# A cross-attention and FP4 feed-forward kernel: P times V as two stacked products, and the last steps written out in an order of their own

## The chip, the cores and the metric

One Trainium2 chip, one core of it. The metric is the device time of one execution in microseconds (us); of the kernel before there are three timed runs. Engines are named as in the profile: PE is TensorE (PEld its loads of stationary operands), DVE is VectorE, ACT is ScalarE, POOL is GpSimd, and SP is SyncE, which here issues nearly all DMAs.

## What is computed

x is 4 x 2048 x 512, the context 4 x 77 x 512. The inputs are float32.

```python
x = x + xattn(layernorm(x), ctx, ctx, mask)       # 16 heads of 32, 77 keys
#   q = x Wq.T + bq; k = ctx Wk.T + bk; v = ctx Wv.T + bv
#   probs = softmax(where(mask, q k.T / sqrt(32), -1e9)); attn = probs v; out = attn Wo.T + bo
x = x + ffn(layernorm(x))
#   fp4_linear quantizes both operands in blocks of 16 along the last axis to FP4 (E2M1)
#   h = silu(fp4_linear(x, w_gate)) * fp4_linear(x, w_up); out = fp4_linear(h, w_down)   # inner width 1408
```

## The kernel before

The 8192 rows of x are cut into 64 tiles of 128 rows. Everything of one tile is done in one pass through seven stages, and seven tiles are in flight at a time: step(e, d, f, a, b, n, m) handles tile s+4 as m (first norm), s+3 as n (queries, scores, softmax), s+2 as b (P times V), s+1 as a (output projection, residual, second norm, quantizing), s as f (gate and up products), s-1 as d (quantizing of h) and s-2 as e (down product and output). In this text step s is the one in which f is tile s.

float32 operands of a product are split in two bf16 halves, HI and LO, and each product is made of three: HI x HI, HI x LO, LO x HI (PRODUCTS). The halves are written by ACT (a copy, HI) and DVE (a subtraction, LO), and turned by a DMA transpose that SP issues.

P times V of a tile is weighted_values(b) on PE. For each of the 16 heads the stationary operand is pT, 77 rows (keys) by 128 columns (queries), and the moving one is 33 columns of v_cur: 32 of V and one of ones, which gives the sum of the row of P. Three matmuls a head make 48 a tile. Its result is in banks 2 to 5, which are also used by the scores and by the third gate/up chunk (banks 2 and 3). DVE reads it in sums_inverse and normalised.

Order of PE in a step: P times V of b, queries of n (48 matmuls), clear_scores, gate/up chunk 0 of f, scores of n, projection of a, down of e, gate/up chunks 1, 2 and 3 of f. Gate/up chunk 0 needs xqT, the turned quantized input of tile f; that is one buffer, so the transpose for the next tile is issued by SP only when chunk 3 of the present one is done (xq_transposed waits for gu_ps). hT, the turned h, is one buffer as well: h_transposed waits for down_done of the tile before.

Each engine has its own instruction list, written out by hand and synchronised by semaphores; within an engine the order of the list holds. Steps 1 to 3 and the last six are unrolled, the others run in a loop (tiles()). In the steps 61 to 65, which have no new tile to take in, the same step function runs with the missing stages left out. A prologue before the steps quantizes the weights, makes K and V and starts the first tiles. V of each of the 4 batches goes to a DRAM scratch and comes back into v_cur at the first step of a batch (load_values), K at the last step of the batch before (load_keys).

Of the kernel before, what the change touches and what calls it, by code (L numbers as in the profile page):

```python
# [11 lines left out]
U32 = mybir.dt.uint32  # L12
# [52 lines left out]
def xattn_fp4_ffn_kernel(nc, x, ctx, mask, wq, bq, wk, bk, wv, bv, wo, bo, w_gate, w_up, w_down, out):  # L65
# [11 lines left out]
    V_LOADS = 16  # L77
# [17 lines left out]
    v_scratch = nc.dram_tensor("v_scratch", [BATCH, KEYS, 2 * D], BF16, kind="Internal").ap()  # L95
    x1_scratch = nc.dram_tensor("x1_scratch", [TILES, P, D], F32, kind="Internal").ap()

    with ExitStack() as es:
# [25 lines left out]
        v_cur = sb("v_cur", [P, 2, HEADS, VW + 1], BF16)  # L124
# [20 lines left out]
        probs = sb("probs", [P, HEADS, KEYS])  # L145
# [29 lines left out]
        w_size, c_size, k_size, v_size = 2 * KC * D, 2 * KC * BATCH * KEYS, BATCH * 2 * GROUPS * KEYS, BATCH * 2 * D  # L175
        ends = [0]
        for size in (w_size, w_size, c_size, k_size, v_size, w_size):
# [5 lines left out]
        v_all = v_room[0:KEYS].rearrange("p (b s d) -> p b s d", b=BATCH, s=2)  # L183
# [21 lines left out]
         s_ps, s_max, exp_done, p0_hi, p1_hi, p0_lo, p1_lo, pv_done, o_ready, o_hi, o_lo, o_ps, x1_done,  # L205
# [3 lines left out]
                 "s_ps s_max exp_done p0_hi p1_hi p0_lo p1_lo pv_done o_ready o_hi o_lo o_ps x1_done "  # L209
# [5 lines left out]
        pT_loaded, p_hi, p_lo = (pT0_loaded, pT1_loaded), (p0_hi, p1_hi), (p0_lo, p1_lo)  # L215
# [32 lines left out]
        DRAIN = TILES + 2  # L248
# [29 lines left out]
        def _(sp):  # L278
# [9 lines left out]
            def load_values(b):  # L288

                sp.dma_start(v_cur[0:KEYS, :, :, 0:DK].rearrange("p s h d -> p (s h) d"),  # L290
                             v_scratch[bass.ds(b, 1)].rearrange("a k (n d) -> (a k) n d", d=DK)).then_inc(v_loaded, 16)
# [15 lines left out]
            sp.dma_start(v_scratch.rearrange("b p w -> p b w"), v_all.rearrange("p b s d -> p b (s d)")).then_inc(kv_stored, 16)  # L307
# [43 lines left out]
            def probabilities(n, pair):  # L351
                after(p_lo[pair], n + 1)
                after(pv_done, GH * n)
                transposed(pT[:, pair].rearrange("p s h t -> p (s h) t"),
                           p_h[:, pair].rearrange("p s w -> p (s w)"), pT_loaded[pair])
# [15 lines left out]
            def xq_transposed(a):  # L371
                after(xq_lo, a + 1)
                after(gu_ps, a * CHUNKS)
                transposed(xqT.rearrange("p s k t -> p (s k) t"), xq_h.rearrange("p s d -> p (s d)"), xqT_loaded)

# [110 lines left out]
            for n in range(TILES - 2, DRAIN + 3):  # L486
                step(n, n - first)
            sp.wait_ge(out_stored, 16 * TILES)

        @block.gpsimd  # L490
        def _(pool):
# [3 lines left out]
            own.did(pool.memset(v_cur[:].rearrange("p s h w -> p (s h w)").bitcast(U32), 0))  # L495
            own.did(pool.memset(probs[:], 0.0))
            own.did(pool.memset(p_h[:].rearrange("p a s w -> p (a s w)").bitcast(U32), 0))
            own.after()
            own.did(pool.memset(v_cur[:, HI, :, DK], 1.0))
# [106 lines left out]

        @block.tensor
        def _(pe):
# [74 lines left out]
            def weighted_values(b):  # L683

                pe.wait_ge(pT0_loaded, 16 * b + 16)
                pe.wait_ge(pT1_loaded, 16 * b + 16)
                for g in range(GROUPS):
                    for s, t in PRODUCTS:
                        for r, ps in enumerate(head_ps):

                            head = g * GH + r
                            ins = pe.matmul(ps[:, g * VW:(g + 1) * VW], pT[0:KEYS, head // PAIR, s, head % PAIR, :],  # L692
                                            v_cur[0:KEYS, t, head, 0:VW], start=s == t, stop=s == LO)
                            if g == GROUPS - 1 and s == LO:
                                ins.then_inc(pv_done, 1)
# [133 lines left out]

        @block.scalar  # L830
        def _(act):
# [19 lines left out]
            for kind, what in plan:  # L851
                if kind == "quant":
                    continue
                if kind == "round":
                    for half in range(2):
                        weight_grid(half, HALF, 2 * what + half + 1)
                    continue
                ps = bank[n % 8]
                act.wait_ge(prep_ps, n + 1)
                if kind == "weight":  # L860
                    which, dst, kc = what
                    ins = act.activation(dst[:, HI, kc, :], ps[:], ACT.Copy, scale=fill_scale[which])
                elif kind == "ctx":
                    ins = act.copy(ctxT[:, HI, what], ps[:, 0:BATCH * KEYS])
                elif kind == "keys":
                    if what == 0:
                        act.wait_ge(bk_ready, 1)
                    ins = act.activation(k_all[:, :, HI, what, :],
                                         ps[:, 0:BATCH * KEYS].rearrange("p (b k) -> p b k", b=BATCH),
                                         ACT.Identity, bias=bk_col[:, what:what + 1])  # L870
                elif kind == "values":
                    ins = act.copy(v_all[:, what, HI], ps[0:KEYS, :])
# [41 lines left out]
            def probabilities_high(n, pair):  # L914
# [3 lines left out]
                         probs[:, pair * PAIR:(pair + 1) * PAIR, :])\  # L918
                   .then_inc(p_hi[pair], 1)

# [52 lines left out]
            def step(e, d, f, a, b, n, m):  # L973
# [14 lines left out]
                if n is not None:  # L988
                    exponentials_second(n, range(2))
                    probabilities_high(n, 0)  # L990
                    exponentials_second(n, range(2, GROUPS))
                if a is not None:
                    normed_second(a)
                if n is not None:
                    probabilities_high(n, 1)
                if f is not None:
# [42 lines left out]
            probabilities_high(0, 0)  # L1039
            masked(1)  # L1040
# [5 lines left out]
            probabilities_high(0, 1)  # L1046
            gate_up_grid(6, 0)
# [7 lines left out]
            probabilities_high(1, 0)  # L1055
            gate_up_grid(7, 0)
            probabilities_high(1, 1)
            q_high(2)
# [16 lines left out]
            probabilities_high(2, 0)  # L1075
            gate_up_high(8, 1)
# [9 lines left out]
            probabilities_high(2, 1)  # L1086
            masked(3)
# [5 lines left out]
            probabilities_high(3, 0)  # L1093
            probabilities_high(3, 1)
            silu_chunk(0, 0)
# [10 lines left out]
            tiles(act, step)  # L1106

        @block.vector
        def _(dve):
# [82 lines left out]
            for kind, what in plan:  # L1192
# [23 lines left out]
                elif kind == "values":  # L1216
                    low(v_all[:, what, LO], ps[0:KEYS, :], v_all[:, what, HI], prep_lo, n + 1)
# [85 lines left out]
            def probabilities_low(n, pair):  # L1303
                dve.wait_ge(p_hi[pair], n + 1)
                high, whole = (p_h[:, pair, HI].rearrange("p (h k) -> p h k", k=P)[:, :, 0:KEYS],
                               probs[:, pair * PAIR:(pair + 1) * PAIR, :])
                low(p_h[:, pair, LO].rearrange("p (h k) -> p h k", k=P)[:, :, 0:KEYS], whole, high,
# [216 lines left out]


# [25 lines left out]
```

## Time and profile before

| | |
|---|---|
| median of 3 runs | 2054.94 us (2054.4 to 2055.07) |
| the profiled execution, its own time | 2054.96 us |
| its span, first to last instruction | 2053.1 us |
| mean granted PE clock | 0.971 |
| busy: PE, PEld, DVE, ACT, POOL | 94%, 59%, 86%, 58%, 22% |
| steps 5 to 60, one step | 28.91 us |
| P times V records (48 a tile) | 87.5 us in all |

The span is 1.9 us shorter than the execution's own time; what lies around it is taken as unchanged. Records of PE are modelled at their ends, so the distance between the starts of two groups is the better measure of what the first one costs.

### The profile page before, as it was taken

To read this page: it belongs to the slowest core of one execution; us is meant where nothing else is said; L and a number is where in the kernel's file an instruction comes from. 1 tells how busy PE (TensorE), PEld (TensorE's weight loads), DVE (VectorE), ACT (ScalarE), POOL (GpSimd) and SP (SyncE) were. 2 spreads that over 40 slices of the span, in tenths; PEclk is the share of its full clock that TensorE was granted. 3 is DMA by queue.
4 is the path that set the end of the run, shared out by engine and by line. 5 is a ranking of instruction groups with operands and counts; after the bars stand their busy time and mean duration, and the time that the engine had idled before them with its cause. 6 is when DMAs were issued, how large, how long until landed. Compare 5 with 4: busy or idle time off the path is not lost.

```text
span 2053.1 us, 50510 instructions
## 1 busy us (share of the span) xinstructions
PE 1931.9 (94%) x18816; PEld 1215.5 (59%) x18816; DVE 1771.6 (86%) x2676; ACT 1198.6 (58%) x2485; POOL 453.2 (22%) x525
## 2 busy tenths in 40 slices
PE   6447999999999999999999999999999999999986
PEld 4235566666666666666666666666666666666543
DVE  7898988888888888888888888988888888888873
ACT  4565665566656665566656665566556665566421
POOL 5563221112211221112111221122111221122110
PEclk9668999999999999999999999999999999999998
DMA  5354566655665556655765566555765566555632
GB/s 168 104 115 99 117 124 148 133 127 131 147 142 124 131 132 146 132 130 128 151 136 124 132 137 146 127 131 127 155 132 125 131 141 145 123 131 124 137 75 54
DMA packets 725826, 264.95 MB, mean 129 GB/s; under 512 B 677682, under 2 KB 678706, under 8 KB 725786
## 3 DMA queue, kind: packets, MB, share of 16 engines
q1 hardware_dynamic: 724202, 264.43, 58.4%
q8 instruction: 23, 0.38, 0.1%
q10 hardware_dynamic: 1584, 0.01, 0.1%
q14 instruction: 17, 0.14, 0.0%
HBM read 65.97 MB, written 34.82 MB: 49 GB/s over the span
## 4 chain that ended last, share of the span: by engine, by line
PE 86%; DVE 6%; DMA 3%; issue 2%; POOL 1%; SPq 1%; ACT 0%; DVEq 0%; POOLq 0%; another core or an unknown queue 0%; ACTq 0%
PE psum L679 43%; PE psum L615 38%; PE psum L692 3%; PE psum L721 2%; DVE h_room L1146 1%; DMA t_room<-halves 1%; DMA ph_room<-h_room 1%; POOL h_room L521 1%; PE psum L710 1%; DVE w_sc L1126 1%; DMA ph_room<-p_h 1%; POOL h_room L525 1%; DVE h_room L1188 1%; DVE wguT L1114 1%; SPq L336 0%
## 5 line engine op out<-in xcount | busy, mean ns | idle before, releaser
L679 PE MATMUL psum<-wguT,t_room 128*128 128x352 bf16 x6144 | 939.6, 313 | 15.9 <-DMA t_room<-halves 10.6
L679 PEld LDWEIGHTS psum<-wguT,t_room 128*128 128x128 bf16 x6144 | 596.3, 98 | 344.2 <-DMA t_room<-halves 10.4
L615 PE MATMUL psum<-wdT,ph_room 128*128 128x512 bf16 x2112 | 471.4, 382 | 13.0 <-DMA ph_room<-h_room 13.0
L542 POOL TENSOR_TENSOR ln_var_eps<-ln_mean_var,eps 128x1 f32<-128x1 f32 x128 | 105.2, 822 | 1198.4 <-DVE ln_mean_var L1261 1011.0
L615 PEld LDWEIGHTS psum<-wdT,ph_room 128*128 128x128 bf16 x2112 | 207.8, 98 | 266.5 <-issue 21.3
L895 ACT ACTIVATE silu_g<-psum 128x352 f32<-128x352 f32 x256 | 117.7, 460 | 421.3 <-PE psum L679 421.3
L901 ACT ACTIVATE probs<-psum,neg_max 128x77 f32<-128x77 f32 x1024 | 245.1, 350 | 3.8 <-DVE neg_max L1299 3.0
L1293 DVE TENSOR_TENSOR h_room<-silu_g,psum 128x352 f32<-128x352 f32 x256 | 132.4, 517 | 80.3 <-ACT silu_g L895 80.3
L926 ACT ACTIVATE t_room<-psum,bq_col 128x128 bf16<-128x128 f32 x256 | 73.2, 368 | 207.1 <-PE psum L615 207.0
L615 PE MATMUL psum<-t_room,wqT 128*128 128x128 bf16 x3072 | 186.7, 222 | 0.2 <-DMA t_room<-halves 0.2
L615 PE MATMUL psum<-woT,t_room 128*128 128x512 bf16 x768 | 179.8, 384 | 1.2 <-DMA t_room<-halves 1.2
L615 PEld LDWEIGHTS psum<-t_room,wqT 128*128 128x128 bf16 x3072 | 176.9, 99 | 0.6 <-issue 0.2
L839 ACT ACTIVATE h_sq<-h_room 128x1408 bf16<-128x1408 f32 (+2 forms) x94 | 108.2, 1151 | 113.0 <-DVE h_room L1146 113.0
L556 POOL TENSOR_TENSOR io_room<-io_room,bo_all 128x512 f32<-128x512 f32 x64 | 83.2, 1300 | 248.1 <-DMA io_room<-in_x_dram 248.1
L1314 DVE TENSOR_TENSOR x_new<-psum,io_room 128x512 f32<-128x512 f32 x64 | 44.3, 692 | 88.2 <-PE psum L615 75.0
L615 PEld LDWEIGHTS psum<-woT,t_room 128*128 128x128 bf16 x768 | 70.8, 99 | 83.4 <-issue 3.9
L1146 DVE SCALAR_TENSOR_TENSOR h_room<-h_room,h_sc 128x1408 f32<-128x1408 f32 x64 | 104.0, 1625 | 2.2
L1160 DVE TENSOR_TENSOR h_room<-h_room,h_sc 128x1408 f32<-128x1408 f32 x64 | 104.0, 1625 | 2.2
L546 POOL TENSOR_SCALAR ln_shift<-ln_mean_var,ln_rstd 128x1 f32<-128x1 f32 x128 | 101.9, 796 | 12.6
L1152 DVE SCALAR_TENSOR_TENSOR h_room<-h_sq,h_room 128x1408 f32<-128x1408 bf16 x64 | 102.0, 1593 | 2.9 <-ACT h_sq L839 2.9
L1114 DVE TENSOR_TENSOR h_room<-h_room 128x1408 bf16<-128x1408 f32 x64 | 103.6, 1619 | 0.0
L1156 DVE SCALAR_TENSOR_TENSOR h_room<-h_sq,h_room 128x1408 f32<-128x1408 bf16 x64 | 103.6, 1618 | 0.0
(103 smaller groups left out, 2459.3 us busy)
## 6 DMA issues: line engine op xcount, KB each, us to landing
io_room<-in_x_dram SPq DMA_DIRECT2D x128, 256.0 KB, 2.8
x_scratch<-x_new SPq DMA_DIRECT2D x64, 256.0 KB, 2.0
x_cur<-x_scratch SPq DMA_DIRECT2D x64, 256.0 KB, 3.0
out_dram<-io_room SPq DMA_DIRECT2D x64, 256.0 KB, 2.4
t_room<-halves SPq DMA_TRANSPOSE x192, 3.2
raw<-in_L_ffn_w_down_dram SPq DMA_DIRECT2D x4, 704.0 KB, 4.2
raw<-in_L_ffn_w_gate_dram SPq DMA_DIRECT2D x11, 256.0 KB, 2.6
raw<-in_L_ffn_w_up_dram SPq DMA_DIRECT2D x11, 256.0 KB, 2.9
```

Source lines behind the costliest of these rows:

```text
L542: own.did(pool.tensor_tensor(var_eps, mean_var[:, 1:2], eps[:], ALU.add))
L615: ins = pe.matmul(dst, left(i), right(j), start=first and n == 0, stop=last and n == len(PRODUCTS) - 1)
L679: ins = pe.matmul(ps[:, 0:CW], left[:, i, kc, :], wguT[:, which, j, kc, cols], start=(kc == 0 and i == j), stop=(kc == KC - 1 and i == LO))
L839: act.activation(dst, val, ACT.Square, scale=GRID_SLOPE).then_inc(done, 1)
L895: act.activation(silu_g[:, c % 2, :], gate_ps[c][:, 0:CW], ACT.Silu).then_inc(silu_done, 1)
L901: ins = act.activation(probs[:, h, 0:KEYS], score_ps[:, r, g, :], ACT.Exp, bias=neg_max[:, h:h + 1])
L1114: return own.did(dve.tensor_tensor(dst, ps, high, ALU.subtract), signal, value)
L1146: step_of(job, dve.scalar_tensor_tensor(blocks(job.val), blocks(job.src), TIES_DOWN, spread(job.sc, 2, job.nb), ALU.mult, ALU.mult), job.d ...
L1152: step_of(job, dve.scalar_tensor_tensor(job.tot, job.sq, GRID_BASE, job.val, ALU.add, ALU.subtract))
L1156: step_of(job, dve.scalar_tensor_tensor(job.tot, job.sq, GRID_BASE, job.tot, ALU.add, ALU.subtract))
L1160: step_of(job, dve.tensor_tensor(blocks(job.res), blocks(job.tot), spread(job.sc, 1, job.nb), ALU.mult), job.done)
L1293: own.did(dve.tensor_tensor(h[:, c * CW:(c + 1) * CW], silu_g[:, c % 2, :], up_ps[c][:, 0:CW], ALU.mult), h_done, f * CHUNKS + (c + 1))
```

## The change

Keys are stacked in the contraction. The stationary operand of a head now has 117 rows: 77 of HI of P (all keys), one of zeros, and 39 of LO of P. In slot HI of p_h the 39 are the LO part of keys 0 to 38, in slot LO those of keys 39 to 76, and both slots have HI of P in their first 77. The moving operand v_cur has in slot HI HI of V and below it HI of V of the first 39 keys, in slot LO LO of V and below it HI of V of the others. Two matmuls a head (32 a tile) then give the same three products.

- ACT: probabilities_again, a second copy of the same 8 x 77 elements for each pair (two a tile). In step() one stands between the last exponentials and normed_second, the other behind probabilities_high(n, 1). Eight more stand in the prologue's list.
- DVE: probabilities_low writes 2 x 39 elements a head rather than 77, into rows 78 to 116 of both slots.
- SP: probabilities(n, pair) waits for p_again too; load_values is four DMAs, with whole rows of 1088 bytes rather than pieces of 64 bytes.
- POOL: one more memset of v_room at the start, and the ones go into v_all.
- The steps from 61 on are written out for every engine (DRAIN is TILES - 3). On PE the projection of tile 62 stands ahead of gate/up chunk 0 of tile 61, P times V of tile 63 behind that chunk, and down(59), down(60), down(61) behind chunk 3 of tiles 61, 62, 63 rather than ahead of chunk 1. The quantized input of tile 63 is turned into xnT, which is free by then.

```diff
-                    for s, t in PRODUCTS:
+                    for s in (HI, LO):
                         for r, ps in enumerate(head_ps):
                             head = g * GH + r
-                            ins = pe.matmul(ps[:, g * VW:(g + 1) * VW], pT[0:KEYS, head // PAIR, s, head % PAIR, :],
-                                            v_cur[0:KEYS, t, head, 0:VW], start=s == t, stop=s == LO)
+                            ins = pe.matmul(ps[:, g * VW:(g + 1) * VW], pT[0:STACK, head // PAIR, s, head % PAIR, :],
+                                            v_cur[0:STACK, s, head, 0:VW], start=s == HI, stop=s == LO)
...
+            def probabilities_again(n, pair):
+                act.copy(p_h[:, pair, LO].rearrange("p (h k) -> p h k", k=P)[:, :, 0:KEYS],
+                         probs[:, pair * PAIR:(pair + 1) * PAIR, 0:KEYS])\
+                   .then_inc(p_again[pair], 1)
...
-                low(p_h[:, pair, LO].rearrange("p (h k) -> p h k", k=P)[:, :, 0:KEYS], whole, high,
+                low(p_h[:, pair].rearrange("p s (h k) -> p h s k", k=P)[:, :, :, LOW_AT:STACK],
+                    whole.rearrange("p h (s k) -> p h s k", s=2), high.rearrange("p h (s k) -> p h s k", s=2),
                     p_lo[pair], n + 1)
...
+                sp.dma_start(whole[0:KEYS, HI], rows[:, HI]).then_inc(v_loaded, 16)
+                sp.dma_start(whole[LOW_AT:STACK, HI], rows[0:LOW_KEYS, HI]).then_inc(v_loaded, 16)
+                sp.dma_start(whole[0:KEYS, LO], rows[:, LO]).then_inc(v_loaded, 16)
+                sp.dma_start(whole[LOW_AT:LOW_AT + rest, LO], rows[LOW_KEYS:KEYS, HI]).then_inc(v_loaded, 16)
...
             tiles(pe, step)
+            LAST = TILES - 1
+            projection(LAST - 1)
+            gate_up_chunk(xqT, 0)
+            weighted_values(LAST)
+            gate_up_chunk(xqT, 1)
+            pe.wait_ge(o_ready, TILES)
+            gate_up_chunk(xqT, 2)
+            gate_up_chunk(xqT, 3)
+            down(LAST - 4)
+            projection(LAST)
+            gate_up_chunk(xqT, 0)
+            gate_up_chunk(xqT, 1)
+            gate_up_chunk(xqT, 2)
+            gate_up_chunk(xqT, 3)
+            down(LAST - 3)
+            gate_up_chunk(xnT, 0)
+            gate_up_chunk(xnT, 1)
+            gate_up_chunk(xnT, 2)
+            gate_up_chunk(xnT, 3)
+            down(LAST - 2)
+            down(LAST - 1)
+            down(LAST)
```

(The waits between these last lines are left out, but for the one for o_ready.) DVE's new list from step 61 on begins like this; tile 60 is LAST - 3:

```diff
+            top(h_job(LAST - 3))
+            scale(h_job(LAST - 3))
+            inverse(h_job(LAST - 3))
+            divide(h_job(LAST - 3))
+            h_chunk(LAST - 2, 0)
+            residual(LAST - 1)
+            first_round(h_job(LAST - 3))
+            second_norm(LAST - 1)
+            second_norm_end(LAST - 1)
+            second_round(h_job(LAST - 3))
+            sums_inverse(LAST)
+            h_chunk(LAST - 2, 1)
+            normalised(LAST)
...
```

## Rows read from the trace of the kernel before

**Rows 1.** The page, part 4: the chain that ended last, by engine.
```profile
PE 86%; DVE 6%; DMA 3%; issue 2%; POOL 1%; SPq 1%; ACT 0%; DVEq 0%; POOLq 0%; another core or an unknown queue 0%; ACTq 0%
```

**Rows 2.** One step: length, busy of PE, PEld, DVE, ACT, POOL; clock, DMA, GB/s.
```profile
1265.90:1294.80 28.90, 28.90 (x291) 18.17 (x290) 25.57 (x39) 17.74 (x38) 5.64 (x7) 1.00 0.61 134
```

**Rows 3.** Timeline of PE, one step: start, us, engine, line, operation.
```profile
1271.81 1.36 PE L692 MATMUL psum<-v_cur,ph_room 77*128 77x33 bf16 x48
1273.02 2.84 PE L615 MATMUL psum<-t_room,wqT 128*128 128x128 bf16 x48
1276.04 3.75 PE L679 MATMUL psum<-wguT,t_room 128*128 128x352 bf16 x24
...
1300.72 1.36 PE L692 MATMUL psum<-v_cur,ph_room 77*128 77x33 bf16 x48
```

**Rows 4.** By tile: loads of 77 and 128 rows, ns min/median/max.
```profile
L692 PEld LDWEIGHTS psum<-v_cur,ph_room x3072: 95/96/151, 133.1 to 1938.3; 77*128 77x128 bf16 x192
...
L615 PEld LDWEIGHTS psum<-t_room,wqT x3072: 95/98/151, 86.9 to 1912.0; 128*128 128x128 bf16 x192
```

**Rows 5.** Timeline of PE in the prologue.
```profile
162.24 1.57 PE L692 MATMUL psum<-v_cur,ph_room 77*128 77x33 bf16 x48
```

**Rows 6.** Timeline of ACT and DVE, one step, around the copies.
```profile
1264.85 0.46 ACT L895 ACTIVATE silu_g<-psum 128x352 f32<-128x352 f32 x1 [2.54 <-PE psum L679]
...
1289.24 0.69 ACT L917 CAST p_h<-probs 128x616 bf16<-128x616 f32 x1
...
1289.93 0.80 DVE L1114 TENSOR_TENSOR p_h<-probs,p_h 128x616 bf16<-128x616 f32 x1
1290.64 0.68 DVE L1126 TENSOR_REDUCE x_sc<-q_room 128x32 f32<-128x512 f32 x1
```

**Rows 7.** Timeline of DVE, same step: two of its waits.
```profile
1273.24 0.26 DVE L1274 RECIPROCAL inv_sum<-psum 128x16 f32<-128x16 f32 x1 [0.21 <-PE psum L692]
...
1277.08 0.87 DVE L1266 SCALAR_TENSOR_TENSOR t_room<-psum,bq_col,t_room 128x128 bf16<-128x128 f32 x3 [0.49 <-ACT t_room L926]
```

**Rows 8.** SP's transpose xqT, by line: one step; then landing in step 3.
```profile
L336 SPq DMA_TRANSPOSE t_room<-halves x1: 1232/1232/1232, 1272.1 to 1272.1; - x1
DMA to landing us min/median/max: 3.1/3.1/3.1
...
DMA to landing us min/median/max: 4.9/4.9/4.9
```

**Rows 9.** The last two such transposes at a batch's end.
```profile
L336 SPq DMA_TRANSPOSE t_room<-halves x2: 1232/1233/1234, 1010.8 to 1012.3; - x2
```

**Rows 10.** Timeline of PE, end of the prologue.
```profile
190.27 10.91 PE L679 MATMUL psum<-wguT,t_room 128*128 128x352 bf16 x72 [1.68 <-DVE h_room L1293]
```

**Rows 11.** Timeline from step 61 on; one piece of the chain.
```profile
1940.56 3.75 PE L679 MATMUL psum<-wguT,t_room 128*128 128x352 bf16 x24 [2.01 <-DMA t_room<-halves]
1944.15 2.75 PE L615 MATMUL psum<-woT,t_room 128*128 128x512 bf16 x12
1946.74 7.29 PE L615 MATMUL psum<-wdT,ph_room 128*128 128x512 bf16 x33
1947.37 0.69 DVE L1314 TENSOR_TENSOR x_new<-psum,io_room 128x512 f32<-128x512 f32 x1 [3.61 <-POOL io_room L556]
1950.86 1.62 DVE L1156 SCALAR_TENSOR_TENSOR h_room<-h_sq,h_room 128x1408 f32<-128x1408 bf16 x1
...
1953.86 10.90 PE L679 MATMUL psum<-wguT,t_room 128*128 128x352 bf16 x72
1967.96 3.75 PE L679 MATMUL psum<-wguT,t_room 128*128 128x352 bf16 x24 [3.20 <-DMA t_room<-halves]
...
2022.35 10.07 PE L615 MATMUL psum<-wdT,ph_room 128*128 128x512 bf16 x33 [4.54 <-DMA ph_room<-h_room]
...
2034.84 5.25 DMA ph_room<-h_room
2040.23 9.66 PE L615 MATMUL psum<-wdT,ph_room 128*128 128x512 bf16 x33 [7.82 <-DMA ph_room<-h_room]
```

More of the change, by code:

```diff
@@ L352, in probabilities @@
                 after(p_lo[pair], n + 1)
+                after(p_again[pair], n + 1)
                 after(pv_done, GH * n)
@@ L487, in _ @@
                 step(n, n - first)
+            LAST = TILES - 1
+            load_residual(LAST)
+            store_x1(LAST - 1)
+            load_x1(LAST - 4)
+            o_transposed(LAST)
+            xq_transposed(LAST - 1)
+            h_transposed(LAST - 3)
+            store_out(LAST - 4)
+            load_x1(LAST - 3)
+            xq_transposed_last()
+            h_transposed(LAST - 2)
+            store_out(LAST - 3)
+            store_x1(LAST)
+            load_x1(LAST - 2)
+            h_transposed(LAST - 1)
+            load_x1(LAST - 1)
+            store_out(LAST - 2)
+            h_transposed(LAST)
+            load_x1(LAST)
+            store_out(LAST - 1)
+            store_out(LAST)
             sp.wait_ge(out_stored, 16 * TILES)
@@ L495, in _ @@
             own.did(pool.memset(v_cur[:].rearrange("p s h w -> p (s h w)").bitcast(U32), 0))
+            own.did(pool.memset(v_room[0:KEYS].bitcast(U32), 0))
             own.did(pool.memset(probs[:], 0.0))
@@ L498, in _ @@
             own.after()
-            own.did(pool.memset(v_cur[:, HI, :, DK], 1.0))
+            own.did(pool.memset(v_all[:, :, HI, :, DK], 1.0))
             own.did(pool.memset(ones_b[:], 1.0))
@@ L1039, in _ @@
             probabilities_high(0, 0)
+            probabilities_again(0, 0)
             masked(1)
@@ L1086, in _ @@
             probabilities_high(2, 1)
+            probabilities_again(2, 1)
             masked(3)
@@ new lines, in _ @@
+            top(x_job(LAST - 1))
+            scale(x_job(LAST - 1))
+            inverse(x_job(LAST - 1))
+            divide(x_job(LAST - 1))
+            h_chunk(LAST - 2, 2)
+            half_low(o_h, o_sb, o_hi, o_lo, LAST)
+            first_round(x_job(LAST - 1))
+            second_round(x_job(LAST - 1))
+            rescale(x_job(LAST - 1))
+            half_low(xq_h, xq, xq_hi, xq_lo, LAST - 1)
+            rescale(h_job(LAST - 3))
+            h_chunk(LAST - 2, 3)
+            tile_out(LAST - 4)
@@ new lines, in _ @@
+            top(h_job(LAST - 2))
+            scale(h_job(LAST - 2))
+            inverse(h_job(LAST - 2))
+            residual(LAST)
+            divide(h_job(LAST - 2))
+            second_norm(LAST)
+            second_norm_end(LAST)
+            h_chunk(LAST - 1, 0)
+            half_low(h_h, hq, h_hi, h_lo, LAST - 3)
+            top(x_job(LAST))
+            scale(x_job(LAST))
+            inverse(x_job(LAST))
+            divide(x_job(LAST))
+            h_chunk(LAST - 1, 1)
+            first_round(x_job(LAST))
@@ new lines, in _ @@
+            h_chunk(LAST, 1)
+            tile_out(LAST - 3)
+            first_round(h_job(LAST - 1))
+            second_round(h_job(LAST - 1))
+            rescale(h_job(LAST - 1))
+            h_chunk(LAST, 2)
+            h_chunk(LAST, 3)
+            top(h_job(LAST))
+            scale(h_job(LAST))
+            half_low(h_h, hq, h_hi, h_lo, LAST - 1)
+            inverse(h_job(LAST))
+            divide(h_job(LAST))
+            tile_out(LAST - 2)
+            first_round(h_job(LAST))
+            second_round(h_job(LAST))
```

124 lines of the change are left out of this document (107 added, 17 removed).

## The prediction, written before the change was run

> **What bounds the kernel now.** I read the chain of waits first: 86% of what ended last is PE [rows 1]. Then one step by windows: in 28.90 us PE has no gap at a granted clock of 1.00 (2.4 GHz), while DVE is busy 25.57 and ACT 17.74 [rows 2]. The timeline of PE puts the same group one step apart at 1271.81 and 1300.72, so a step is 28.91 us [rows 3], and the chain of waits shows the same period from step 5 on. Between the starts there, P times V costs 1.21 us (1271.81 to 1273.02) and the queries run behind it; gate/up chunk 0 starts at 1276.04. What PE doesn't do shortens every step, as long as nothing takes PE's place. Only the first four steps, the ends of batches, and the steps from 61 on have waits of PE.
>
> **Two products for three, in the steps.** 48 matmuls take 1.20 to 1.21 us, 25.1 ns each. 16 fewer are 0.40 us a step. The question is what one of 117 rows costs. No row shows 117 rows with 33 columns. From below: 25.1 ns, as with 77. From above, nearest: the load of a 77-row operand is recorded with a median of 96 ns and of a 128-row one with 98 [rows 4]; if the whole difference came into the distance, 26.7 ns, and the gain is 1.21 - 32 x 0.0267 = 0.35 us. Farthest: the queries, 128 rows with 128 columns, 2.84 us for 48 [rows 3], 59 ns, and then there is a loss. I take 25.1: at the low clock of the prologue 48 of them took 1.57 us against 1.36 at the full one [rows 3, 5], so the price is hardly set by the array's own pace, and 33 columns are far from those 128. Something below nothing is excluded, as no work is left out but the 16 matmuls and no distance under 25 ns is seen for whole-array matmuls.
>
> The Trainium skill, "TensorE: Matmul & The Clock Gate", section "LDWEIGHTS (loading the stationary operand)", says that the time of a load goes by its columns and that the number of rows doesn't matter. The rows show 2 ns between 77 and 128 rows. By that rule the gain is 0.40 us a step, by the 2 ns it is 0.35; over 56 steps that is 2.8 us apart.
>
> Is the 0.40 kept? Four covers, each worked out in the step of the rows.
> - xqT. SP issues it at 1272.1 when chunk 3 is done, it lands 3.1 later, 1275.2 [rows 8], and gate/up chunk 0 starts at 1276.04 [rows 3]: 0.8 of margin. P times V and the queries are what covers it, so 0.40 of it goes and 0.4 is left. In step 3 it landed only after 4.9 [rows 8].
> - DVE idles 0.21 before sums_inverse and 0.49 before q_low [rows 7], 0.70 in all, and needs 0.40 of it. The stretches behind are measured from PE's later chunks and keep their distance.
> - ACT gets two copies of 0.69 us [rows 6]. The first delays normed_second, which now ends as the copy at 1289.24 starts, to about 1290.0; DVE wants its result at 1290.64. Both together come out of the 2.54 us that ACT waits for gate/up chunk 1 [rows 6]; 1.1 is left. Behind the first stand normed_second and probabilities_high(n, 1), behind the second the silu of chunk 1. SP, which now waits for p_again, gets both before DVE's own LO part.
> - probabilities_low has 624 elements for 616 at 0.80 us [rows 6]: nothing, at most 0.01. The DMA transposes have the same size.
>
> So step for step: P times V stands on PE-bound ground in steps 5 to 60, 56 x 0.40 = 22.5 us. In step 1 it gains 0.4 too. In steps 2 to 4 PE waits behind it for a transpose, and the gain becomes wait: 0. At the three ends of batches SP is late; the last transpose is issued at 1012.3 [rows 9] rather than right behind chunk 3, so PE's start moves by perhaps 0.15 of the 0.40: 0.8 us less in all.
>
> **Prologue.** It is paced by DVE, and ACT has gaps where the new copies stand, but for the last: probabilities_again(3, 1) stands right ahead of the silu whose chunk PE waits for at 190.27 [rows 10]. +0.7 us. The longer memset of POOL is hidden by the first weight load, for which PE waits until 10.07. load_values is four DMAs for one on SP's queue; behind them wait load_x1, load_x and store_x1, which have us of room, and v_loaded is asked for 15 us later: 0 (bounds 0 and +0.5 for all batches).
>
> **The last steps.** On the clock of before, from the end of chunk 3 of tile 60 at 1937.2 [rows 11], which hold for all of this part: a chunk is 3.59, a projection 2.59, a down product 7.12, by the distances of their starts. Projection(62) fills part of the 2.01 that PE waits today; chunk 0 of 61 still starts at 1940.56 and ends at 1944.15; P times V 0.8; chunk 1 waits for DVE's h_chunk, ends 1949.0. Chunk 2 now waits for normalised(63). DVE stands at residual(62) until POOL's sum is there, 1947.37 as today, and then has a residual, two passes of 1.62, and six small ones ahead, 6.2 us: 1953.6, PE idle 4.6. Then two chunks, down(59), projection(63) and chunk 0 of 62 to 1974.1; 1.3 of wait for h_chunk(62, 0); three chunks, down(60), chunk 0 of 63, 1.3 again, three chunks: 2008.9. Down(61) ends at 2016.0. Only then may SP turn h of tile 62, 5.4 with the waits on both sides, and 0.2 ahead: down(62) starts at 2021.7 (2022.35 today). It runs at the lower clock after such a wait, 10.07, as today, to 2031.7. The transpose of tile 63 goes out at once, since DVE has had its h ready since about 2025.5; today DVE finishes it only after tile_out(62), and it goes out at 2034.84. Down(63) starts at 2037.3 in place of 2040.23. That is 2.9 earlier, the 0.4 of P times V of tile 63 included; I take 2.7. What is late next is the one hT buffer, twice.
>
> Its bounds: PE's clock fell after idling 4.54 and 7.82 and didn't after 3.20 [rows 11]. If it falls after the new 4.6 too, 2.6 us go (half of what a down product loses is the size: 10.07 less 7.12 is 2.9, the other 2.5), and nearly nothing is left. If it stays up in one of the two waits of 5.6 at the end, 2.6 more come. So 0 to 5.3.
>
> **Sum.** 2054.96 - 22.5 - 0.4 + 0.8 + 0.7 - 2.7 = 2030.9. The profiled execution is 0.02 over the median, so 2030.8 us, 1.2% less.
>
> **Rivals.**
> 1. The transpose becomes the bound. xqT's margin goes from 0.8 to 0.4. If it lands 0.6 later than now, as half-way to step 3's 4.9 it may when the step is shorter, half of the gain in the steps is wait: 2042. For it: PE waited for it in steps 3 and 4. Against: in every looped step it landed in 3.0 to 3.3.
> 2. Slower: 117 rows cost more than 77 because the operand fills the array as the queries' does. 32 x 59 ns is 1.89 us, +0.68 a step, +38 in 56: 2054.96 + 38 + 0.7 - 2.3 = 2091. It decides from 1.21 / 32 = 37.8 ns. Against: 2 ns between the loads.
> 3. ACT's copies eat the gain: if they take as much longer as 1.1 us in all, silu, and behind it DVE, run late, and PE's chunk 3 begins to wait; DVE's waits of 0.70 are nearly used up too. A third of the gain is gone, and the last steps give nothing: about 2041. If all of it is gone, no change, 2054.
> 4. The change does in the last steps less than it says, all else holds: 2033.6; or more: 2028.3. These are inside the forecast.
>
> **Chances.** Forecast with its bounds (2027 to 2037): 0.74. Rivals 1 and 3 at 2038 to 2050: 0.14; no change within 0.2% (about 4 us, what a measurement of this kernel can tell from none): 0.04; slower, rival 2 or the like: 0.06; more gain than 2027: 0.02. The range for 8 in 10 runs from 2026.5 (all bounds low: no 0.8, no 0.7, 5.3) to 2040, which takes in 26.7 ns (+2.8), nothing from the last steps (+2.7) and the nearer part of rivals 1 and 3. Faster 0.90, same 0.04, slower 0.06.
>
> **What would show it.** The record of a step: the distance of the P times V group to the queries 0.80 to 0.85, the step 28.51, PE without idle in it. If the distance is over 1.2, rival 2. If PE's idle before chunk 0 names the transpose of halves, rival 1; if chunk 3 or 1 waits for DVE or ACT, rival 3. At the end: the idle before gate/up chunk 2 of tile 61 near 4.6 with DVE's psum read as its releaser, and the last two down products starting 15.6 apart. I am wrong if the step is under 28.4 or over 28.7, or if the time behind step 60 is longer than 116 us as now.

## The result, and the profile after

| | before | after |
|---|---|---|
| median of the runs, us | 2055.01 (2054.4 to 2055.58) | 2031.49 (2031.19 to 2034.46) |
| ratio to before, 95% interval | | 0.9889 (0.9872 to 0.9906) |
| profiled execution: time, span, us | 2054.96, 2053.1 | 2031.19, 2029.3 |
| start of step 5 (P times V) | 316.87 | 316.78 |
| from there to the end of gate/up chunk 3 of step 60 | 1620.31 | 1599.41 |
| behind that | 115.9 | 113.1 |

The kernel is 1.1% faster: 2031.49 us, where 2030.8 was forecast, with 2026.5 to 2040 as the range. The last three rows split the 23.8 us by which the two spans differ: 0.1 in the prologue, 20.9 in the steps, 2.8 behind them. The prediction had 0.3 lost, 21.7 and 2.7 gained. The middle one of these differences repeats within some 0.3 us in the other traces. The other two are one draw each, and the traces further down give them other sizes.

The chain of waits of after, shares of the span by engine. PE's share is the one of before [rows 1]:

```profile
PE 86%; DVE 6%; DMA 3%; issue 2%; POOL 1%; SPq 1%; ACT 1%; DVEq 0%; POOLq 0%; another core or an unknown queue 0%; ACTq 0%
```

One step by windows (window, length, busy us with instructions of PE, PEld, DVE, ACT and POOL, granted clock, DMA share, GB/s), against [rows 2]:

```profile
1262.50:1291.01 28.51, 28.35 (x276) 17.75 (x275) 25.56 (x39) 18.83 (x39) 5.62 (x7) 1.00 0.63 136
```

The step is 28.51 us for 28.91. ACT is busy 1.1 us more; over exactly one step it has 39 instructions for 37, the two copies (the window of [rows 2] happens to hold 38). DVE is as busy as before.

The timeline of PE over one step (start, duration, engine and line, operation, the idle time in front in brackets), against [rows 3]:

```profile
1288.06 0.96 PE L737 MATMUL psum<-v_cur,ph_room 117*128 117x33 bf16 x32
1288.87 2.84 PE L660 MATMUL psum<-t_room,wqT 128*128 128x128 bf16 x48
1291.64 0.31 PE L755 MATMUL psum<-zeros_b 32*128 32x308 bf16 x4
1291.89 3.75 PE L724 MATMUL psum<-wguT,t_room 128*128 128x352 bf16 x24
```

P times V begins at 1288.06 and the queries at 1288.87: 0.81 us for 32 matmuls, 25.3 ns each, where it was 1.21 for 48. No line has idle time in front. The 0.16 us by which PE's busy time falls short of the step stands in front of the projection, where one of its 12 matmuls has no record; the second trace of the kernel before has the same 0.16 there.

The groups of weight loads, by line (count, then the median of one in ns between its extremes), against [rows 4]:

```profile
L737 PEld LDWEIGHTS psum<-v_cur,ph_room x2048: 95/96/152, 133.0 to 1924.0; 117*128 117x128 bf16 x187
```

A 117-row operand loads in 96 ns, as the 77-row one did.

The timelines of ACT and DVE around the new copies, against [rows 6, 7]:

```profile
1304.08 0.72 ACT L1010 CAST p_h<-probs 128x616 bf16<-128x616 f32 x1
1309.62 0.46 ACT L982 ACTIVATE silu_g<-psum 128x352 f32<-128x352 f32 x1 [1.60 <-PE psum L724]
...
1289.25 0.26 DVE L1407 RECIPROCAL inv_sum<-psum 128x16 f32<-128x16 f32 x1
1292.92 0.87 DVE L1399 SCALAR_TENSOR_TENSOR t_room<-psum,bq_col,t_room 128x128 bf16<-128x128 f32 x3 [0.33 <-ACT t_room L1019]
1305.78 0.80 DVE L1246 TENSOR_TENSOR p_h<-probs,p_h 128x624 bf16<-128x624 f32 x1
```

Here the 0.40 us is paid: ACT's wait for chunk 1 went from 2.54 to 1.60, and DVE's two waits from 0.21 and 0.49 to nothing and 0.33. ACT's busy time rose by 1.09 (17.74 to 18.83) for two copies of 0.72, so the records of neighbours overlap by some 0.17 each (my estimate from these numbers). The LO part has 624 elements for 616 and still takes 0.80. The transpose of xqT is issued at 1288.33 and lands 3.0 later; the margin to chunk 0 at 1291.89 is 0.56, of the 0.8 of [rows 3, 8].

The end of the second batch, timeline of PE, against [rows 9]:

```profile
1002.47 1.01 PE L737 MATMUL psum<-v_cur,ph_room 117*128 117x33 bf16 x32 [0.29 <-DMA ph_room<-p_h]
1003.73 2.85 PE L660 MATMUL psum<-t_room,wqT 128*128 128x128 bf16 x48 [0.25 <-DMA t_room<-halves]
```

P times V waits for the transpose of P, and the queries for the transpose of the normed input.

The last steps, timeline of PE, against [rows 11]:

```profile
1919.66 3.74 PE L724 MATMUL psum<-wguT,t_room 128*128 128x352 bf16 x24 [0.53 <-DMA t_room<-halves]
1924.58 3.75 PE L724 MATMUL psum<-wguT,t_room 128*128 128x352 bf16 x24 [0.39 <-DVE h_room L1426]
1931.95 8.78 PE L724 MATMUL psum<-wguT,t_room 128*128 128x352 bf16 x48 [3.62 <-DVE q_room L1411]
1955.20 10.91 PE L724 MATMUL psum<-wguT,t_room 128*128 128x352 bf16 x72 [1.18 <-DVE h_room L1426]
...
2001.51 9.79 PE L660 MATMUL psum<-wdT,ph_room 128*128 128x512 bf16 x32 [5.47 <-DMA ph_room<-h_room]
2016.78 8.99 PE L660 MATMUL psum<-wdT,ph_room 128*128 128x512 bf16 x33 [5.48 <-DMA ph_room<-h_room]
```

These are the waits that the prediction named, in its order: gate/up chunk 2 of tile 61 waits 3.62 for DVE to read a psum, then 1.18 (a second 1.18 is not shown), then 5.47 and 5.48 for the one hT buffer, with the down products starting 15.27 apart. One more thing stands in them: the two chunks behind the 3.62 took 8.78 us, where two at the full clock take some 7.3 (24 matmuls 3.75, the next 24 3.59 more), so the clock fell for a part of them: the granted clock over 1931.95 to 1940.70 is 0.83.

### The profile page after: what moved, and what is told of

It is laid out like the page before. It is cut to its first block, busy times and chain, and to the rows that moved or that the text cites. A ratio compares the mean times of both kernels' runs of the same rounds, so it can differ in the third digit from the quotient of the medians.

```text
span 2029.3 us, 48669 instructions
## 1 busy us (share of the span) xinstructions
PE 1898.9 (94%) x17724; PEld 1192.0 (59%) x17792; DVE 1770.0 (87%) x2676; ACT 1266.9 (62%) x2613; POOL 448.8 (22%) x526
## 4 chain that ended last, share of the span: by engine, by line
PE 86%; DVE 6%; DMA 3%; issue 2%; POOL 1%; SPq 1%; ACT 1%; DVEq 0%; POOLq 0%; another core or an unknown queue 0%; ACTq 0%
PE psum L724 44%; PE psum L660 38%; PE psum L737 2%; PE psum L766 2%; DMA t_room<-halves 1%; DVE h_room L1278 1%; SPq L345 1%; PE psum L755 1%; POOL h_room L560 1%; DVE w_sc L1258 1%; POOL h_room L564 1%; DMA ph_room<-h_room 1%; DVE wguT L1246 1%; DVE h_room L1320 0%; DMA q_room<-in_L_xattn_Wk_dram 0%
## 5 line engine op out<-in xcount | busy, mean ns | idle before, releaser
L982 ACT ACTIVATE silu_g<-psum 128x352 f32<-128x352 f32 x256 | 117.4, 459 | 380.2 <-PE psum L724 377.1
L660 PE MATMUL psum<-woT,t_room 128*128 128x512 bf16 x705 | 165.7, 384 | 12.0 <-issue 10.1
L1246 DVE TENSOR_TENSOR p_h<-probs,p_h 128x624 bf16<-128x624 f32 x128 | 103.9, 812 | 0.0
L1288 DVE SCALAR_TENSOR_TENSOR h_room<-h_sq,h_room 128x1408 f32<-128x1408 bf16 x64 | 103.6, 1618 | 0.1
L1258 DVE TENSOR_REDUCE h_sc<-h_room 128x88 f32<-128x1408 f32 x64 | 102.6, 1603 | 0.1
```

Of the source, the lines that this page charges most:

```text
L660: ins = pe.matmul(dst, left(i), right(j), start=first and n == 0, stop=last and n == len(PRODUCTS) - 1)
L982: act.activation(silu_g[:, c % 2, :], gate_ps[c][:, 0:CW], ACT.Silu).then_inc(silu_done, 1)
L1246: return own.did(dve.tensor_tensor(dst, ps, high, ALU.subtract), signal, value)
L1258: step_of(job, dve.tensor_reduce(job.sc[:, 0, 0:job.nb], blocks(job.src), AX_X, ALU.max, apply_absolute_value=True))
L1288: step_of(job, dve.scalar_tensor_tensor(job.tot, job.sq, GRID_BASE, job.tot, ALU.add, ALU.subtract))
```

## The experiments

Nine more kernels were run, and the two compared ones once more. Times are medians, ratios are to the kernel before as run beside them, with their 95% interval. "Step" is the distance of two P times V groups in the trace.

**The two halves of the change, each alone.** `e1_products` is the changed kernel with the loops running to the end as before:

```
-        DRAIN = TILES - 3
+        DRAIN = TILES + 2
```

together with the removal of the steps written out behind each engine's loop. `e2_drain` is the kernel before with only these written-out steps added, and three products as before.

> The stacked products with all that belongs to them (copy, loads of V, memset), but the steps from 61 on as in the kernel before. If the terms add up as the two traces split them, this takes what the steps gave and not what the end gave: 2055.0 less 21.0 is 2034, a step of 28.51 us, and some 115.5 us behind step 60 (0.4 less than before for the last tile's P times V). Rival: the two parts depend on each other, and the end is shorter or longer by over 1 us than that, or the steps before 5 come out otherwise.

> The kernel before, three products a head, with the steps from 61 on written out in the new order. By my account a step stays at 28.91, and the end is 113.5 us rather than 115.9: 2052.5. The gap of PE ahead of gate/up chunk 2 of tile 61 is 3.6 to 4.6. Rival: the order at the end gives nothing by itself (2055), because the gap there pulls the clock of PE down.

Measured: the products alone 2036.73 us, ratio 0.9908 (0.9891 to 0.9925), step 28.51; that is 2.7 over what was expected, and the time behind step 60 is 118.5 for the 115.5 expected. The order alone 2050.88 us, ratio 0.9978 (0.9968 to 0.9988), step 28.91. They take 0.92% and 0.22% off, 1.14% together, and the whole change gave 1.11%: within these intervals (0.17 and 0.10 points either way) the halves don't disturb each other. By the ratios the order is worth 4.5 us, by the two profiled executions of before and after it was 2.8 with the 0.4 of tile 63's products in it. The reason for the difference is in the timeline of PE behind the loops of `e1_products`:

```profile
1919.07 5.43 PE L698 MATMUL psum<-wguT,t_room 128*128 128x352 bf16 x24 [2.40 <-DMA t_room<-halves]
1976.91 5.43 PE L698 MATMUL psum<-wguT,t_room 128*128 128x352 bf16 x24 [3.20 <-DMA t_room<-halves]
```

24 of these matmuls take 3.75 us at the full clock and took 5.43 here, after waits of 2.40 and 3.20. In the execution of before that the prediction read, the clock stayed up after 2.01 and 3.20 [rows 11]. So the old order has waits that cost the clock in some executions and not in others. Behind step 60 the four traces with the old order take 115.9, 117.4 (`before_again`), 121.1 (`e3_rows117`) and 118.5 (`e1_products`); the five with the new order and no further edit there take 113.1, 114.6 (`after_again`), 113.3 (`e2_drain`), 113.2 (`e5_third`) and 113.8 (`e6_keys`). With the 0.4 of tile 63's products counted alike, the means are some 4.8 apart, 4.4 of it by the order, and that agrees with the 4.5 of the ratios. The first trace of before is the shortest of its kind, which is why the one pair shows only 2.8.

**What a product of 117 rows costs.** `e3_rows117` is the kernel before with all its 48 products made over 117 rows, 40 of which lie beyond the 77 keys.

```
-  ins = pe.matmul(ps[:, g * VW:(g + 1) * VW], pT[0:KEYS, head // PAIR, s, head % PAIR, :],
-                  v_cur[0:KEYS, t, head, 0:VW], start=s == t, stop=s == LO)
+  ins = pe.matmul(ps[:, g * VW:(g + 1) * VW], pT[0:117, head // PAIR, s, head % PAIR, :],
+                  v_cur[0:117, t, head, 0:VW], start=s == t, stop=s == LO)
```

> The kernel before, 48 products a tile, but each with 117 rows rather than 77 (the 40 more are zeros on both sides; the result is the same). If rows cost nothing, a step stays at 28.91 and the time at 2055. If a load pays by its rows as the 2 ns between the records of 77 and 128 rows would allow, 48 x 1.6 ns is 0.08 a step and 4.3 in all: 2059. If 117 rows cost what the queries' 59 ns are, 48 x 34 ns is 1.6 a step: 2147.

Measured: 2055.92 us, ratio 1.0001 (0.9991 to 1.0012), step 28.91. Forty rows more cost nothing that can be measured, in 3072 products. Rival 2 is out.

**How much more the steps would give.** `e4_one` is the changed kernel with one product per head; the LO half of P times V is left out.

```
-                    for s in (HI, LO):
+                    for s in (HI,):
```

> The new kernel with the second product of each head left out (16 matmuls a tile; the LO half of V and half of the LO part of P are missing from the result). It asks how much more PE can give before another takes its place. DVE has 0.33 us of wait left ahead of q_low and the turned xqT some 0.45 ahead of chunk 0; 16 matmuls less are 0.40 us. If DVE's 0.33 is the next bound, a step is 28.51 less 0.33, 28.18, and PE shows a wait; if neither binds, 28.11, 2009; if the transpose binds, PE idles for it ahead of chunk 0.

Measured: 2009.65 us, ratio 0.9776 (0.9757 to 0.9796), step 28.11 to 28.16 with most at 28.12. The next 0.40 is kept all but for 0.01, so rival 1 is out for the change itself, which asked for only the first 0.40. But xqT is now close to its limit. Two steps of `e4_one` by the timeline of PE:

```profile
1248.91 0.31 PE L755 MATMUL psum<-zeros_b 32*128 32x308 bf16 x4
1249.16 3.75 PE L724 MATMUL psum<-wguT,t_room 128*128 128x352 bf16 x24
...
1277.03 0.31 PE L755 MATMUL psum<-zeros_b 32*128 32x308 bf16 x4
1277.31 3.75 PE L724 MATMUL psum<-wguT,t_room 128*128 128x352 bf16 x24
```

In the first xqT lands at 1248.99 (issued at 1245.99, 3.0 to landing), 0.17 ahead of the chunk, where the changed kernel has 0.56. In the second it lands at 1277.21, 0.10 ahead, and the chunk starts 0.28 behind the clearing and not 0.25. So the scatter of the steps up to 28.16 fits a transpose that has begun to bind now and then. My own expectation that DVE would end the gain at 28.18 was wrong: q_low starts 1.03 behind chunk 0 in this trace (1250.19) as in the one of after (1292.92 behind 1291.89), so DVE gave the whole 0.40 there, though its recorded wait was 0.33. The ends of the batches shrank less than the plain steps: their six steps are 28.52 to 28.96, 1.3 us less than in the changed kernel where six plain ones lose 2.3.

**What ACT's copies cost.** `e5_third` has a third copy for each pair of heads, into a buffer that nobody reads:

```
+            def probabilities_third(n, pair):
+                at_least(act, third_done[pair], n - 4)
+                act.copy(third[:, pair].rearrange("p (h k) -> p h k", k=KEYS),
+                         probs[:, pair * PAIR:(pair + 1) * PAIR, 0:KEYS]).then_inc(third_done[pair], 1)
```

> The new kernel with a third copy of P's rows by ACT for each pair in every step (two copies of 0.7 us more a step, into a tile that nobody reads). In the new kernel ACT waits 1.60 us for gate/up chunk 1. If ACT's copies are covered, as I hold, the wait shrinks to 0.2 to 0.5 and a step stays at 28.51 (2031.5). If they are what eats gain, the step grows: by my rival 3 some 0.1 to 0.5 us, 2037 to 2060.

Measured: 2033.27 us, ratio 0.9891 (0.9871 to 0.9912), step 28.51. The timeline of ACT shows what paid:

```profile
1310.82 0.46 ACT L984 ACTIVATE silu_g<-psum 128x352 f32<-128x352 f32 x1 [0.39 <-PE psum L726]
```

The wait went from 1.60 to 0.39, so two more copies took 1.2 us of it and the step is unchanged. The change's copies are covered, with room for these two more and 0.39 to spare. Rival 3 is out for the steps; what the copies do ahead of step 5 is told under the prologue below.

**The ends of the batches.** In the changed kernel the three steps at each end are, by the distances of P times V, 28.94 and 29.00, 28.97 and 28.97, 28.94 and 28.92: 2.7 us over six steps of 28.51. Before they were 29.12 and 29.01, 29.34 and 28.99, 29.28 and 28.91: 1.2 over steps of 28.91. So 1.5 of the gain is lost there, not 0.8. The timeline of SP at one such end (SPq is SP's queue):

```profile
994.45 0.82 SPq L289 DMA_DIRECT2D k_cur<-k_scratch  x1
997.30 0.34 SPq L369 DMA_DIRECT2D mask_raw<-in_mask_1x1xSxS_bk_dram  x1
997.91 2.00 SPq L345 DMA_TRANSPOSE ph_room<-p_h  x1
```

After the issue of the keys (994.45) SP stands until they have landed, issues the mask at 997.30, and only then the transpose of P's second half. `e6_keys` turns that round:

```
-                    if keys is not None:
-                        after(k_loaded, 16 * (keys + 1))
-                    load_mask(n + 1, j + 1 if keys is None else 0)
...
                     probabilities(n, 1)
+                if keys is not None:
+                    after(k_loaded, 16 * (keys + 1))
+                    load_mask(n + 1, 0)
```

> The new kernel, and in the last step of a batch SP issues the turning of the second pair of P ahead of its wait for the new keys and of the load of the mask, rather than behind both. The three ends of batches cost 2.7 us over plain steps in the new kernel (1.2 in the one before). If SP's wait for the keys is the cause, each falls to 28.5 to 28.6 and the time by 2.2 to 2.7: 2029. Rival: the turned P is late for another reason (DVE), and nothing changes.

Measured: 2030.02 us, ratio 0.9874 (0.9858 to 0.9891). The timeline of SP:

```profile
538.86 1.02 SPq L289 DMA_DIRECT2D k_cur<-k_scratch  x1
540.14 2.54 SPq L345 DMA_TRANSPOSE ph_room<-p_h  x1
542.87 0.44 SPq L369 DMA_DIRECT2D mask_raw<-in_mask_1x1xSxS_bk_dram  x1
```

Every step from 5 on, ends of batches included, is now 28.51 or 28.52: the 2.7 is gone. What SP no longer does ahead of the transpose is the wait for the keys, some 2.0 us (995.27 to 997.30), and the issue of the mask, 0.34; the edit moved both, and the wait is by far the larger. In the medians only about 1.5 of the 2.7 arrives, and the intervals of the two ratios overlap, so it is the steps that show this gain and not the time. The profiled execution reaches step 5 at 318.56, 1.8 later than after's; the spread of the prologue is told below.

**The waits of the last steps.** Two kernels take one each of the waits that the prediction had named. `e7_room` is the changed kernel with h of tile 62 turned into the room of pT, which is free by then, so that it no longer waits for down(61):

```
+        h2T = ph_room[:, 0:2 * IC * P].rearrange("p (s k t) -> p s k t", s=2, k=IC)
...
+            def h_transposed_next_to_last():
+                after(h_lo, TILES - 1)
+                after(pv_done, GH * TILES)
+                transposed(h2T.rearrange("p s k t -> p (s k) t"), h_h.rearrange("p s w -> p (s w)"), hT_loaded)
...
-            down(LAST - 1)
+            down(LAST - 1, h2T)
```

`e8_sums` moves DVE's read of the psum of tile 63's P times V to right behind the h of chunk 0 of tile 61, ahead of the residual of tile 62:

```
+            sums_inverse(LAST)
+            normalised(LAST)
...
-            sums_inverse(LAST)
...
-            normalised(LAST)
```

> The new kernel, and h of tile 62 is turned into the room of pT, which is free after P times V of tile 63, so that the turn needn't wait for down(61). By my account down(62) starts 2.4 us earlier, the wait of 5.5 ahead of it becomes 3.2, and the end comes 3.5 us earlier if the clock does the same, up to 6 if PE's clock no longer falls there: 2025.5 to 2028. Rival: the last tile's own chain through DVE binds and less than 1 us comes out.

> The new kernel, and DVE reads P times V of tile 63 (sums_inverse, normalised) right behind h_chunk(61, 0) rather than behind residual(62) and two passes of h. PE's wait ahead of gate/up chunk 2 of tile 61 (3.6 us, DVE's read as its releaser) should be gone. If that wait is on the path to the end, the time falls by about 4: 2027.5. Rival: it is given back at the next waits for DVE's chunks (1.2 each), and under 1 us is left.

Measured: `e7_room` 2024.92 us, ratio 0.9848 (0.983 to 0.9866); `e8_sums` 2026.55 us, ratio 0.9862 (0.9845 to 0.9878). The timelines of PE, first of `e7_room`:

```profile
2000.67 7.28 PE L671 MATMUL psum<-wdT,ph_room 128*128 128x512 bf16 x32 [2.89 <-DMA ph_room<-h_room]
2012.35 8.97 PE L671 MATMUL psum<-wdT,ph_room 128*128 128x512 bf16 x33 [4.40 <-DMA ph_room<-h_room]
```

and of `e8_sums`:

```profile
1923.79 10.91 PE L724 MATMUL psum<-wguT,t_room 128*128 128x352 bf16 x72 [0.39 <-DVE h_room L1426]
```

In the first the waits of 5.47 and 5.48 are 2.89 and 4.40. In the second the three chunks run through and the 3.62 is gone. Both gains reach the end, so both waits stood on the path, as the prediction had them: the time behind step 60 is 108.3 in `e7_room` and 106.9 in `e8_sums`, for 113.1. In `e8_sums` that is more than the 3.6 that was taken away; some 1.4 more is the fall of the clock behind it (8.78 for the two chunks in after), and 1.0 came with last products of 9.13 and 8.66 for 9.79 and 8.99.

**All three together.** `e9_all` has the edits of `e6_keys`, `e7_room` and `e8_sums`, and nothing else.

> The new kernel with three edits together: the turning ahead of the wait for keys at the ends of batches, the room of pT for h of tile 62, and DVE's read of tile 63 early. If they add: ratios 0.9874, 0.9848 and 0.9862 against the new kernel's 0.9889 make 0.0015 + 0.0041 + 0.0027, so 0.981 of the kernel before, 2015 to 2018 us. Rival: the two edits at the end overlap, since both shorten the same last 113 us, and the sum stays over 2020.

Measured: 2016.96 us (2015.88 to 2019.0), ratio 0.9809 (0.9793 to 0.9824), as expected if the three add up. This beats both kernels: 1.9% under before and, by the medians, 0.7% under the changed one. Behind step 60 it takes 101.6. Its last two products, by the timeline of PE:

```profile
1993.02 8.97 PE L672 MATMUL psum<-wdT,ph_room 128*128 128x512 bf16 x32 [2.88 <-DMA ph_room<-h_room]
2004.72 8.88 PE L672 MATMUL psum<-wdT,ph_room 128*128 128x512 bf16 x33 [2.72 <-DMA ph_room<-h_room]
```

Here down(62) takes 8.97 after a wait of 2.88; in `e7_room` the same product took 7.28 after 2.89. The granted clock is 0.81 in the first and 1.00 in the second.

**The same two kernels once more**, to learn how far one profiled execution speaks for the others.

> The kernel before as it is, profiled once more, for the spread of its parts between executions. Up to step 5 (316.87 us in the first trace) the kernels with three products came to 313.6 and 314.5, those with two to 314.9 to 316.8. If that is the spread of any kernel, this one's start of step 5 differs from 316.87 by up to 3 us; the steps stay at 28.91 within 0.02; the end may differ by its clock.

> The new kernel as it is, profiled once more. Step 5 started at 316.78 us in its first trace. If the prologue's length is spread and not the change's doing, this execution has another, within 313 to 317; steps stay at 28.51, and the end at 113 within 2.

Measured: 2055.34 us with a span of 2053.6, and 2031.6 with 2029.8. Start of step 5 at 316.20 and 315.92; the steps from there to the end of step 60's chunk 3 1620.0 and 1599.3; behind them 117.4 and 114.6. The three parts differ by 0.3, 20.7 and 2.8, as they did in the first pair. The timeline of PE in the last steps of the second execution of before:

```profile
1939.62 5.08 PE L679 MATMUL psum<-wguT,t_room 128*128 128x352 bf16 x24 [2.02 <-DMA t_room<-halves]
1968.35 5.43 PE L679 MATMUL psum<-wguT,t_room 128*128 128x352 bf16 x24 [3.20 <-DMA t_room<-halves]
1997.47 5.17 PE L679 MATMUL psum<-wguT,t_room 128*128 128x352 bf16 x24 [3.23 <-DMA t_room<-halves]
```

and of after:

```profile
1930.87 10.14 PE L724 MATMUL psum<-wguT,t_room 128*128 128x352 bf16 x48 [3.55 <-DVE q_room L1411]
2016.01 10.21 PE L660 MATMUL psum<-wdT,ph_room 128*128 128x512 bf16 x33 [5.44 <-DMA ph_room<-h_room]
```

The same kernel before, after waits of the same length as in the first execution, now has the lower clock for a part of 24 matmuls three times: granted 0.73, 0.69 and 0.72. In the first execution it had 1.00 after all three. What the old order loses at the end is therefore not one number; 115.9 and 117.4 are two draws.

## Why the prediction was right, point by point

**What bounds the kernel.** PE without gaps in a step, so what PE doesn't do comes off: 0.40 us from PE, 0.40 from the step, and with `e4_one` again 0.40. Right.

**The price of 117 rows.** 25.1 ns was taken between 25.1 and 26.7; the trace has 25.3 and `e3_rows117` the ratio 1.0001. The argument from the nearest rows (loads of 96 and 98 ns) held, and the rule of the Trainium skill ("TensorE: Matmul & The Clock Gate", "LDWEIGHTS (loading the stationary operand)") that rows don't matter agrees with both numbers here.

**The four covers.** All held. The size that was off is ACT's: the wait was to fall to 1.1 and fell to 1.60. A copy overlaps its neighbours by some 0.17, which durations added up one by one don't show; for two copies that explains 0.35 of the 0.5. DVE's 0.30 was 0.33, xqT's margin of 0.4 was 0.56.

**The ends of the batches** are the one term that was wrong in kind. I had the late transpose of xqT move PE's start by 0.15 of the 0.40 each time, 0.8 in all. It was 1.5, and by the transpose of P and then the one of the normed input, which stand behind SP's wait for the keys. The failed step is that I took the last of SP's transposes at [rows 9] as the late one; all of them are late by the same wait, and the first that PE needs is P's. `e6_keys` shows it.

**Prologue.** 0.7 lost was said, less the 0.4 of step 1; the first pair of profiles gave 0.1 gained. That one difference says little: the start of step 5 lies at 316.87 and 316.20 for before, 316.78 and 315.92 for after, and at 313.64 and 314.50 in `e2_drain` and `e3_rows117`, whose prologues do what before's does. But much of the spread is there ahead of the first P times V, whatever the kernel (131.35 to 134.07). Counted from that group, step 5 starts after 181.9 to 183.8 us in the four traces with three products a head, and after 183.8 to 185.0 in the seven with two (`e4_one` and `e5_third`, which change this stretch as well, are left out): 1.9 more on average. One part of it is the same in every trace. The timeline of PE in the changed kernel, against [rows 10]:

```profile
190.41 12.59 PE L724 MATMUL psum<-wguT,t_room 128*128 128x352 bf16 x72 [2.58 <-DVE h_room L1426]
```

The wait ahead of these three chunks is 1.51 to 1.68 in the four traces with three products, and the chunks take 10.91, at a granted clock of 1.00. In all nine traces with the new copies it is 2.58 to 3.09 and they take 12.46 to 12.59, at 0.86 in the trace of after. From the P times V group ahead of them to the chunks it is some 0.6 longer, where the prediction's two terms make 0.3, by the copy in front of the silu as it said; the other 1.7 is the clock, which the prediction left out. A part of these 2.2 us comes back by step 5, since PE waits for DVE and transposes in steps 2 to 4 anyway. No run took the copies out while it kept the two products, so that the copy is what lengthens the wait is read from ACT's timeline and not tested.

**The last steps.** 2.7 was said with bounds 0 and 5.3. Both pairs of profiles gave 2.8, but the ratio of `e2_drain` gave 4.5 (2.5 to 6.6 by its interval) and the means over all traces 4.8 with tile 63's 0.4, so the term was too small: the first trace of before, from which it was worked out, is the one in which the old order lost least. Two of its terms were off in opposite ways. The wait before chunk 2 was 3.62, not 4.6: the residual of tile 62 began 2.1 ahead of chunk 1's end, not 1.6, and DVE took 5.7 us (1926.20 to 1931.89) instead of 6.2. Against that the clock fell for a part of the two chunks behind it, 8.78 us in place of some 7.3; this was one end of the bounds (at 2.6) and not in the sum. In all seven traces with this wait, 3.54 to 3.85 long, the clock fell: the two chunks took 8.78 to 10.14, 1.4 to 2.8 more than at the full clock. So down(61) ended 79.9 behind the end of step 60 and not 78.8, down(63) began at 100.6 and not 100.1, and the end came out even because down(63) took 8.99 and not the 9.66 of before. The starts of the last two were 15.27 apart instead of 15.6, since the first took 9.79 and not 10.07. That 2.7 came out at 2.8 in the first pair is therefore luck in good part; the waits and their releasers are right, and `e7_room` and `e8_sums` show the large ones to be on the path by shortening or removing them. What the prediction lacked is that the waits of the kernel before are a draw too: it took "the clock didn't fall after 3.20" [rows 11] as a property of that wait. `before_again` has the fall after 2.02 and 3.20.

**The sum.** For the profiled execution 2030.9 was said and 2031.19 measured. The 0.3 between them is 0.8 less gained in the steps (0.7 of it at the ends of batches) against 0.4 in the prologue and 0.1 at the end. The median lies another 0.3 above the profiled one. Over all traces the split is another one: some 20.8 gained in the steps, 4.8 at the end, 1.9 lost in the prologue, which makes 23.7 where the medians give 23.5. The steps came out as said, by the mechanism that was said. The other two terms were both too small, by some 2.1 and 1.6 us in opposite directions and both through PE's clock behind short waits, and that they cancel is luck: the forecast hit to 0.7 us with errors larger than that inside.

## What to carry to other kernels

When one engine has no gap in a step, the removal of its instructions is worth their start-to-start distance times the count, once each other engine's and each transfer's wait in that step is written down and found to be at least as long. Rows of a stationary operand that stand empty are then free room for stacking, as the 40 rows were here. A queue that waits for one late transfer delays everything issued behind it, so look at what stands first behind the wait and not at what lands last. A list of the remaining waits, with who releases each, is a list of further changes: two in the last steps and one at the ends of batches gave another 0.7%. And where PE waits, as in a prologue or at the end, price each wait with the clock up and with the clock down behind it, and read more than one trace before taking a wait's cost as known.

## What the runs showed of the hardware that was not expected

- The granted clock after a short wait of PE isn't a function of the wait alone. After 3.20 us, 24 gate/up matmuls took 5.43 in `before_again` and in `e1_products` and 6.50 in `e3_rows117`, and the clock stayed up in the first execution of before. After 2.02 they took 5.08 in `before_again`. After 2.88 and 2.89 the same down product took 8.97 in `e9_all` and 7.28 in `e7_room`. What PE did directly ahead of the wait was the same in each pair; what decides between them stays open.
- Of the spread in the start of step 5 (313.64 to 318.79 over all the traces) 2.7 us are there before any step: the first P times V starts between 131.35 and 134.07. The latest are 134.07 (`e9_all`), 133.53 (`before_again`) and 133.52 (`e6_keys`), so the kernel before has a late one too. `e6_keys` and `e9_all`, which have the latest starts of step 5 but an edit that should not touch the prologue, take 185.0 and 184.7 from there, where the other five with two products take 183.8 to 184.6. Whether the edit has a part in the rest wasn't tested.
